# One more level of a triangular inverse masked and turned by VectorE, with one half-precision product less on TensorE

## The reference

```python
def step(S, x):
    qt, kt, vt, bt, gt = x
    S = S * jnp.exp(gt)[..., None, None]
    kv = jnp.einsum('bhk,ebhkv->ebhv', kt, S)
    delta = (vt[None] - kv) * bt[..., None]
    S = S + kt[None, :, :, :, None] * delta[..., None, :]
    ot = jnp.einsum('bhk,ebhkv->ebhv', qt * scale, S)
    return (S, ot)
_, o = jax.lax.scan(step, S0, xs)
```

## Time and profile before

| what | value |
|---|---|
| median of 3 runs | 854.57 us (850.92 to 857.94) |
| the profiled execution, its own time | 855.27 us |
| its span, first to last instruction | 853.3 us |
| mean granted TensorE clock | 0.988 of full speed |
| busy: TensorE, VectorE, GpSimd, ScalarE | 789.5, 641.0, 334.3, 311.6 us |
| the loop of the recurrence | from about 510 to 785 us of the span |

### The profile page before, as it was taken

One profiled execution on the slowest core, in us unless ns is written; L12 is line 12 of the kernel. 1 busy time (PEld: TensorE's weight loads), 2 busy tenths in 40 slices (PEclk: granted clock), 3 DMA queues, 4 the chain that ended last, 5 costly groups with the idle time before them and its releaser, 6 DMA issues.

```text
span 853.3 us, 23384 instructions
## 1 busy us (share of the span) xinstructions
PE 789.5 (93%) x10074; PEld 528.6 (62%) x10074; DVE 641.0 (75%) x1345; ACT 311.6 (37%) x547; POOL 334.3 (39%) x340
## 2 busy tenths in 40 slices
PE   2998999999999999999999997899999999998698
PEld 1453444444566657875444445898999988997243
DVE  6999999996788857542863527888888888883485
ACT  1231112120122230114454623565665664653342
POOL 5231110000011131000375235887887886871640
PEclk9999999999999999999999998999999999999899
DMA  8600000022000007000009653455455445421452
GB/s 247 205 0 1 0 2 0 1 50 65 9 2 1 2 3 269 1 1 1 3 15 391 246 220 92 122 133 146 133 136 145 137 123 138 130 59 40 135 171 72
DMA packets 64079, 77.82 MB, mean 91 GB/s; under 512 B 23572, under 2 KB 46790, under 8 KB 63973
## 3 DMA queue, kind: packets, MB, share of 16 engines
q1 hardware_dynamic: 58853, 55.15, 23.5%
q0 software_dynamic: 5120, 21.14, 6.9%
HBM read 51.82 MB, written 24.39 MB: 89 GB/s over the span
## 4 chain that ended last, share of the span: by engine, by line
PE 67%; DVE 24%; issue 3%; ACT 2%; POOL 1%; DMA 1%; SPq 1%; DVEq 0%; ACTq 0%; POOLq 0%
PE bank L787 14%; PE bank L870 8%; PE bank L1062 4%; PE bank L895 4%; PE bank L583 4%; DVE rows L1557 3%; PE bank L597 3%; DVE rows L1686 3%; DVE rows L1559 3%; PE bank L802 3%; PE bank L886 2%; PE bank L799 2%; PE bank L919 2%; PE bank L955 2%; PE bank L650 2%
## 5 line engine op out<-in xcount | busy, mean ns | idle before, releaser
L787 PE MATMUL bank<-W,xT 128*128 128x512 f32 x280 | 124.2, 596 | 0.7 <-ACT big L1141 0.7
L787 PEld LDWEIGHTS bank<-W,xT 128*128 128x128 f32 x280 | 52.0, 190 | 60.2 <-issue 57.9
L1378 POOL TENSOR_TENSOR cnt_r<-cnt_r,ident_sb 125x125 fp32r<-125x125 f32 x10 | 11.4, 1142 | 173.8 <-ACT cnt_r L1127 173.8
L561 PE MATMUL bank<-W,xT 128*125 128x512 f32 x160 | 78.2, 603 | 0.0
L1457 POOL TENSOR_TENSOR W<-big,bdec 64x256 f32<-64x256 f32 x80 | 64.2, 803 | 5.0
L583 PEld LDWEIGHTS bank<-rows 128*126 128x126 f16 x360 | 43.5, 135 | 34.7 <-issue 24.2
L1692 DVE TENSOR_SCALAR rows<-iota_sb,tC 128x625 f16<-128x625 f16 x180 | 56.2, 377 | 10.5 <-PE bank L583 10.5
L583 PE MATMUL bank<-rows 128*126 128x313 f16 x360 | 58.9, 299 | 4.2 <-DVE rows L1692 4.1
L1557 DVE TENSOR_SCALAR rows<-iota_sb,gbp 125x180 f16<-125x180 f16 x160 | 56.1, 351 | 0.0
L1559 DVE TENSOR_SCALAR rows<-iota_sb,gbp 125x180 f16<-125x180 f16 x160 | 50.2, 314 | 0.0
L571 PE MATMUL bank<-rows 125*128 125x360 f16 x160 | 42.3, 318 | 5.1 <-DVE rows L1559 3.3
(11 more groups left out here) (336 smaller groups left out, 1904.7 us busy)
## 6 DMA issues: line engine op xcount, KB each, us to landing
big<-qkv_slots SPq DMA_DIRECT2D x40, 256.0 KB, 3.5
rows<-step_rows SPq DMA_DIRECT2D x40, 128.0 KB
rows<-gam_rows SPq DMA_DIRECT2D x40, 128.0 KB, 3.7
big<-qkv_slots SPq DMA_DIRECT2D x40, 128.0 KB, 2.9
o_slots<-big SPq DMA_DIRECT2D x40, 128.0 KB, 2.7
big<-qkv_slots SPq DMA_DIRECT2D x40, 64.0 KB, 2.8
x_all<-in_x SPq DMA_DIRECT2D x10, 224.0 KB
out<-tC SPq DMA_DIRECT2D x10, 224.0 KB
```

Of the source, the lines that this page charges most:

```text
L561: last = mm(dst, xT[:, k, t * P:(t + 1) * P], W[:, w, k, :], start=(k == 0), stop=(k == KC - 1 and bias is None))
L787: last = mm(bank[:, b0, :], xT[:, k, t * P:t * P + 128], W[:, w, k, :], start=(k == 0), stop=(k == KC - 1))
```

## The change

The constant FLIP goes from 3 to 2, and all that is derived from it follows:

```diff
 LEVELS = 5
-FLIP = 3
+FLIP = 2
 SEGS = [(0, 4), (4, 4), (8, 2)]
```

## The result

The kernel after takes 859.96 us (median of 7 runs, 858.75 to 861.5) against 854.2 us before on the same chip (7 runs): a ratio of 1.0081, 95% interval 1.006 to 1.0102; by the medians it is 5.8 us slower. (A ratio here is taken from the single runs, and can differ by up to 0.2% from the quotient of the two medians.) On another chip it took 860.13 us against 856.21, a ratio of 1.0036 (1.0021 to 1.0051). One execution of each kernel there, 1324 and 1156 us at a granted clock of 0.57 and 0.66, isn't part of that ratio. So the change costs 0.4 to 0.8%, 3.9 or 5.8 us by the medians. The kernel after hardly differs between the two chips; the kernel before does, and it also scatters more (850.7 to 857.9 us on the first chip). The last experiment bears on why. The forecast was 864.6 us, with a range of 856 to 870.

A forecast was written before the change was run, and what follows sets the result against it. The chain of waits through VectorE's scan bounds the kernel: 8 x 0.70 + 9 x 0.54 + 1.8 + 0.5 = 12.8 us, less 2.5, rounded to 10, on 855.27 us; less 0.7 gives 864.6 us, range 856 to 870.

The forecast's parts named there:

- What bounds the kernel: In the recurrence loop, the wait that ends last counts; between TensorE's pieces the chain passes VectorE's scan and ScalarE's copy.
- Rival B: TensorE's stream alone sets the pace: removing the product saves 0.27 us a unit, 5.4 us in all, 849.2 us; chance 0.08.
- The product that goes: TensorE's 16 matmuls for M in each of 20 units: they cost 0.27 us a unit, 5.4 us in all.
- Mask, copy and `level_up(2)`: After `level_up(1)` starts: level 2's mask at 0.66 us, ScalarE's copy of TM at 1.42, `level_up(2)` at 2.50 (was 2.01).
- The floor: TensorE's own earliest `level_up(3)`, by way of `second_fix`: 5.27 us after `level_up(1)`, up from 4.78.
- The transpose: One more VectorE operation a unit, behind level 2's mask: no cost at `level_up(2)`, but the scan starts 0.54 us later.
- The port: The scan waits for GpSimd's third operation of line 1457 and takes 1.65 us, 0.16 more, in 8 units.
- Rival A: The scan starts before GpSimd's third operation of line 1457, in 8 units: 3.4 us less, 861.2 us; chance 0.26.
- The even unit: An undisturbed unit of the loop takes 13.0 to 13.2 us, was 12.50.
- The first two units: In units 0 and 1 the scan directly follows the mask and comes 0.9 us later, 1.8 us for both.
- What is given back: TensorE's gaps without a semaphore, about 9 us over the loop, partly fall into new idle time: 2.5 us off.
- Rival C: TensorE's gaps without a semaphore come to 5 us more and none is hidden: about 872 us; chance 0.10.

The follow-up runs named there:

- The last experiment: The kernel before with one more load of 256 KB a unit, read by nobody: 860.67 us, ratio 1.0052.
- the serial run: The kernel before with level 2's mask waiting for TM and ScalarE's copy waiting for the mask, product kept, no transpose: 862.17 us, ratio 1.0063.
- the second run: The kernel after once more, unchanged, on another chip: 860.13 us, ratio 1.0036 of the kernel before.

## Why the prediction was right or wrong

- **What bounds the kernel: right.** The path of waits inside a unit sets the pace of the kernel after, not TensorE's share of 93%. In the pattern unit of the kernel before the chain that ended last stays on TensorE from `level_up(1)` to `level_up(3)` (621.62 to 626.61), so the scan's path, which the prediction took for the longer one, only ties with it there; in the kernel after the chain goes through the scan. Rival B, a gain of 5.4 us, is out: `level_up(2)` waits for ScalarE's copy.
- **The product that goes: right in size (0.27 us a unit), wrong in what it is worth.** Taken alone out of the kernel before it is worth 7 us, mostly through gaps. Put back into the kernel after it leaves the even unit as it is; the 4.3 to 4.5 us that this run takes more lie in gaps and in the comparison of two chips.
- **Mask, copy and `level_up(2)`: right within 0.04 us.** The floor that they set for `level_up(3)` over `second_fix` was put at 5.27 us, below the scan's path at 5.60, so the scan was said to decide. The runs bear that out. The 5.54 us of the serial run count from the product that the change takes away, 0.27 us more, and are the same floor; in the kernel after the chain goes through the scan, and TensorE stands idle for 0.29 us before `level_up(3)`.
- **The transpose: right that it costs at the scan** (scan at 2.35 us, as forecast). Alone, in the kernel before, it costs 0.1 us a unit, since the scan's place beside GpSimd counts for more than 0.3 us of delay. In the change it comes on top of the later mask, and there it and the longer scan make up the 0.4 us from TensorE's own path to the scan's (5.49 to 5.92 us), an estimate from two kernels that differ in the product too.
- **The port: right in its direction, in too few units.** GpSimd's third operation came 0.07 us earlier (2.23, not 2.30 us), so the scan lost 0.35 us to it and not 0.43: 1.57 us. The scan took 1.49 us or more in 14 of the 17 units from unit 2 on, where 8 were forecast to wait; the kernel after runs more evenly. Rival A is out; the scan's median is 1.54 us. The lock that the Trainium skill describes (SBUF — State Buffer, section SBUF: two separate sides), in which whichever of the two engines' operations starts first keeps the shared ports for the whole instruction, agrees here as well, and with `lower16` and `pairs` (up to 1.52 and 1.15 us beside GpSimd, 0.69 and 0.42 without), which the prediction didn't look at.
- **The even unit: right**, 13.1 us of 13.0 to 13.2.
- **The first two units: too low.** They cost 27.65 us between the first and the third copy before and 30.44 after: 2.8 us, where 1.8 were forecast; the first copy stands 0.4 us earlier in its span, which gives part of that back.
- **What is given back: this is the term that was mis-sized.** It was taken as 2.5 us, for gaps hidden by the new idle time. From unit 2 to 18 the loop grew by 211.14 - 207.16 = 4.0 us, while 16 even units grew by 16 x 0.62 = 9.9: 5.9 us were given back (6.8 with the trace of the second run in place of the first). Some 5 us of it (6 in the second run) are TensorE's own idle time without a semaphore, 6.4 us before and 1.4 (0.4) after. The source of the term was misread too: the 11.1 us before line 870 hold the weight loads beside the matmuls, whose own idle time there is 3.4 us. Whether the gaps were hidden in the new idle time or didn't arise can't be told, since a gap inside a wait for a semaphore leaves no row of its own. Rival C (more gaps) went the wrong way.
- **The total: inside the range, but nearer to a rival.** With 6 to 7 in place of 2.5 the sum is 12.8 - 6.4 = 6.4 us, and 5.8 were measured. By the two traces the first copy comes 0.4 us earlier, units 0 and 1 take 2.8 more, units 2 to 17 take 4.0 more, unit 18 takes 0.25 more, and what lies behind the last copy 0.9 less, a term that the prediction doesn't have: 5.8 us in all. By its time alone the run is nearer to rival A (861.2 us) than to the forecast; only the length of the scans tells them apart.

The wait of ScalarE for the mask was not taken away in any run: the two would then read the same PSUM banks at once. What it costs alone stays untested.

## What to carry to other kernels

Where work moves from one engine to another inside a loop, price the path from product to product, and price the neighbours too: a VectorE operation with two SBUF inputs and GpSimd's operation of that moment took turns here (a scan of 1.2 us lasted up to 1.6), and an operation moved away from one overlap can land in the next. An average period that is longer than the even one hides a second price, here mostly TensorE's gaps; a change that slows the even units may pay part of it back there (5.9 of 9.9 us here), and one that takes instructions away may win more than its own duration (7 us here for 20 x 0.27 = 5.4).

## What the runs showed of the hardware that wasn't expected

- `lower16` takes 0.69 us alone and 0.73 to 1.52 us beside GpSimd; `pairs` 0.42 and 1.15. By this, shortening a unit's path by 0.53 us (the kernel without the product) made its even unit 0.19 us longer.
- The kernel before scatters by 7 us and more from run to run and by 2.5 us in its median from chip to chip (854.2 to 856.7), while the kernel without its product, with hardly any gaps, stays within 1.7 us (848.1 to 849.8, only four runs). That its scatter is its gaps is likely, but wasn't measured by itself.
